# Three products of rounded parts in place of one fp32 product for the output projection of three batches

## The reference

```python
DIM, HEADS, DHEAD, CTX_DIM = (256, 16, 64, 192)
def _attn(x, ctx, Wq, Wk, Wv, Wo, bo):
    q = (x @ Wq).reshape(b, n, HEADS, DHEAD)
    ...
    attn = jax.nn.softmax(sim, axis=-1)
    out = jnp.einsum('bhij,bjhd->bihd', attn, v).reshape(b, n, INNER)
    return out @ Wo + bo
h = _ln(x, g1, be1)
x = _attn(h, h, Wq1, Wk1, Wv1, Wo1, bo1) + x
...
x = a * jax.nn.gelu(gate, approximate=False) @ W2 + b2 + x
```

## Time and profile before

| | us |
|---|---|
| median of 3 runs | 2043.34 (2043.1 to 2043.39) |
| the profiled execution | 2042.06 |
| its span | 2040.3 |

### The profile page before, as it was taken

One profiled execution on the slowest core, in us unless ns is written; L12 is line 12 of the kernel. 1 busy time (PEld: TensorE's weight loads), 2 busy tenths in 40 slices (PEclk: granted clock), 3 DMA queues, 4 the chain that ended last, 5 costly groups with the idle time before them and its releaser, 6 DMA issues.

```text
span 2040.3 us, 31825 instructions
## 1 busy us (share of the span) xinstructions
PE 2028.6 (99%) x12500; PEld 1387.7 (68%) x12500; DVE 1385.3 (68%) x2124; ACT 1159.7 (57%) x1851; POOL 1416.4 (69%) x745
## 2 busy tenths in 40 slices
PE   8999999999999999999999999999999999999999
PEld 7665665666565566665655666566558999888888
DVE  6477677666767785578678566757777898754453
ACT  5566577544557675255667544657665666533332
POOL 2699799975979998679799867979895576300000
PEclk9999999999999999999999999999999999999999
DMA  7300000001000000010000001000010530000100
GB/s 229 124 7 21 6 7 16 6 6 47 17 11 6 16 6 6 1 63 6 6 6 22 6 1 52 6 6 1 22 47 16 145 84 1 1 21 22 42 11 31
DMA packets 46566, 58.74 MB, mean 29 GB/s; under 512 B 5969, under 2 KB 40401, under 8 KB 45265
## 3 DMA queue, kind: packets, MB, share of 16 engines
q1 hardware_dynamic: 46416, 56.71, 8.9%
HBM read 38.88 MB, written 17.83 MB: 28 GB/s over the span
## 4 chain that ended last, share of the span: by engine, by line
PE 99%; ACT 1%; DVE 0%; DMA 0%; issue 0%; SPq 0%; ACTq 0%
PE score L494 22%; PE score L477 18%; PE score L603 9%; PE score L481 6%; PE score L425 5%; PE attn_project L617 4%; PE attn_project L589 4%; PE score L559 4%; PE attn_project L425 4%; PE first_score L451 4%; PE attn_project L528 3%; PE score L437 3%; PE score L528 2%; PE attn_project L451 2%; PE first_score L518 2%; PE attn_project L437 1%
## 5 line engine op out<-in xcount | busy, mean ns | idle before, releaser
L1316 POOL TENSOR_TENSOR acc<-acc,pT 128x1024 f32<-128x1024 f32 x384 | 914.6, 2382 | 55.4 <-POOL acc L1316 0.9
L1100 ACT ACTIVATE pT<-score 128x1024 f32<-128x1024 f32 x512 | 525.7, 1027 | 102.8 <-PE score L481 59.1
L477 PE MATMUL score<-qk 64*128 64x512 f32 x3072 | 456.2, 399 | 1.5 <-ACT oT L1111 0.9
L494 PE MATMUL score<-pT,vT 128*64 128x512 f32 x2016 | 446.5, 595 | 0.0
L780 DVE TENSOR_REDUCE nmax<-first_score 128x1 f32<-128x512 f32 x512 | 347.9, 679 | 3.5 <-PE first_score L451 1.4
L780 DVE TENSOR_REDUCE nmax<-attn_project 128x1 f32<-128x512 f32 x512 | 347.1, 678 | 0.0
L477 PEld LDWEIGHTS score<-qk 64*128 64x128 f32 x3072 | 257.1, 184 | 120.7 <-ACT pT L1100 67.9
L494 PEld LDWEIGHTS score<-pT,vT 128*64 128x64 f32 x2016 | 139.1, 137 | 289.4 <-issue 251.8
L1313 POOL TENSOR_TENSOR acc<-pT 128x1024 f32<-128x1024 f32 x64 | 154.0, 2406 | 150.3 <-ACT pT L1100 150.3
L802 DVE RECIPROCAL sums<-sums 128x512 f32<-128x512 f32 (+1 forms) x65 | 214.4, 3299 | 57.5 <-ACT sums L1125 56.9
L481 PE MATMUL score<-shift,pick 64*128 64x512 f32 x1024 | 205.5, 391 | 0.0
(11 more groups left out here) (160 smaller groups left out, 3056.1 us busy)
## 6 DMA issues: line engine op xcount, KB each, us to landing
xres<-x_middle SPq DMA_DIRECT2D x10, 512.0 KB, 3.7
xres<-in_x SPq DMA_DIRECT2D x4, 1024.0 KB, 7.6
raw_qk<-in_L_xattn_Wq SPq DMA_DIRECT2D x32, 128.0 KB, 2.2
raw_qk<-in_L_xattn_Wk SPq DMA_DIRECT2D x32, 128.0 KB, 2.4
raw_v<-in_L_xattn_Wv SPq DMA_DIRECT2D x8, 512.0 KB, 4.1
keys_all<-keys SPq DMA_DIRECT2D x1, 4096.0 KB, 12.1
values_all<-values SPq DMA_DIRECT2D x1, 4096.0 KB, 12.4
out_x<-xres SPq DMA_DIRECT2D x7, 512.0 KB, 2.9
```

Source lines behind the costliest of these rows:

```text
L477: e.matmul(bank, qk[P % 2][r, 2 + h, keys], qk[P % 2][r, w, queries], start=(part == 0), stop=False)
L494: last = e.matmul(banks[bank][head * DH:(head + 1) * DH, :], vT[:, v_slot(D, jt), c0:c0 + DH], pT[:, jt, head, :], start=(jt == 0), stop=( ...
L1100: e.activation(pT[:, jt].rearrange("p h n -> p (h n)"), SC[R % 2][:, :], ACT.Exp).then_inc(s.exponential, 1)
L1316: e.tensor_tensor(total, total, pT[:, jt], ALU.add).then_inc(s.probs_added, 1)
```

## The change

The output tiles of batches 0 to 2 are computed as three fp32r products of rounded parts, 24 products a tile in place of 8 in fp32. For that:

- `Wo1` is split once. ScalarE rounds a quarter of it in each of chunks 0 to 3 (`wo1_made`, in ring entries of `oT` that are not yet in use), VectorE subtracts (chunks 1 to 4) and leaves the rest in `wo1`'s own place. SP stores the rounded part in DRAM and loads it at the start of each later batch into `wv`, the place of the split value weights, which is free between two value projections; the second `split_wv` of a batch, in chunk n = 3, waits until the output tiles are done.
- The output's parts take the places of probabilities: `oT_parts[j]` for tile j of a slot are pT's tiles 0 and 1, 2 and 3, 4 and 5, and 0 and 1 again. ScalarE rounds (`split_oT`, three tiles ahead of `write_oT`, the fourth after the slot's other work and once tile 0 is multiplied). GpSimd subtracts, between its adds of the same chunk. Where the batch wraps round the ring a part is made in two pieces (`ring_pieces`).
- In the slot the output tiles now stand last, behind the qk projection.
- The last batch keeps the fp32 product (`out1_whole`), for which SP loads `Wo1` again.

```diff
@@ buffers
-            ("wo1", [PAIRS, DIM], F32))
+            ("wo1", [PAIRS, DIM], F32R))
+        _, *places = overlay(("oT_kept", [PRING, N], F32),
+                             *((f"oT_part{n}", [PAIRS, PART], F32R) for n in range(6)))
+        oT_parts = (places[0:2], places[2:4], places[4:6], places[0:2])
+        wo1_hi = wv[:, :, :, :].rearrange("p w k n -> p (w k n)")
...
+        _, wo1_made = overlay(("oT_first", [PRING - 2, N], F32), ("wo1_made", [PAIRS, DIM], F32R))
@@ slot
-            if b and n in (1, 2):
-                between += [("out1", b - 1, TPC * (n - 1) + t) for t in range(TPC)]
...
-            return jobs
+            return jobs + [("out1", *tile, through[i % len(through)]) for i, tile in enumerate(out1_tiles(C))]
+
+        def out1_tiles(C):
+
+            b, n = divmod(C, BC)
+            return [(b - 1, TPC * (n - 1) + t) for t in range(TPC)] if b and n in (1, 2) else []
+
+        def ring_pieces(b):
+
+            first = PAIRS * b % PRING
+            m = min(PAIRS, PRING - first)
+            return [(slice(first, first + m), slice(0, m))] + [(slice(0, PAIRS - m), slice(m, PAIRS))] * (m < PAIRS)
@@ TensorE
+            def out1(b, t, bank):
+                weights = (wo1_hi, wo1[:, :, :].rearrange("p q n -> p (q n)"))
+                need.wait_ge(s.wo1_hi, 16 * (b + 1))
+                need.wait_ge(s.wo1_lo, 4)
+                need.wait_ge(s.oT_hi, TILES * b + t + 1)
+                need.wait_ge(s.oT_lo, TILES * b + t + 1)
+                bank_free(bank)
+                for i, (o, w) in enumerate(TERMS):
+                    for p in range(PAIRS):
+                        last = e.matmul(banks[bank][:, 0:DIM], oT_parts[t % TPC][o][:, p, :],
+                                        weights[w][:, p * DIM:(p + 1) * DIM],
+                                        start=(i == p == 0), stop=(i == 2 and p == PAIRS - 1))
...
@@ ScalarE
+            def split_oT(C, b, t):
+
+                j = t % TPC
+                need.wait_ge(s.oT_scaled, BC * (b + 1) - (1 if t < TPC else 0))
+                need.wait_ge(s.attended, TILES * C + 2 * j + 1)
+                need.wait_ge(s.probs_added, (TILES - 1) * C + max(2 * j, 1))
+                if j == 3:
+                    need.wait_ge(s.out1_product, TILES * b + t - j + 1)
+                for there, pairs in ring_pieces(b):
+                    last = e.copy(oT_parts[j][0][:, pairs, :], oT[:, there, t * PART:(t + 1) * PART])
+                last.then_inc(s.oT_hi, 1)
...
+                if C < 4:
+                    split_wo1(C)
+                for tile in out1_tiles(C)[0:3]:
+                    split_oT(C, *tile)
                 write_oT(C)
                 whole_array(slot(C))
+                for tile in out1_tiles(C)[3:]:
+                    split_oT(C, *tile)
@@ GpSimd, split_wv
+                need.wait_ge(s.out1_product, D // 2 * TILES if D % 2 else 0)
@@ GpSimd
+            def split_oT(C, b, t):
+
+                j = t % TPC
+                hi, lo = oT_parts[j]
+                need.wait_ge(s.oT_hi, TILES * b + t + 1)
+                need.wait_ge(s.attended, TILES * C + 2 * j + 2)
+                need.wait_ge(s.probs_added, (TILES - 1) * C + 2 * j + 1 if j < 3 else 0)
+                for there, pairs in ring_pieces(b):
+                    last = e.tensor_tensor(lo[:, pairs, :], oT[:, there, t * PART:(t + 1) * PART],
+                                           hi[:, pairs, :].bitcast(F32), ALU.subtract)
+                last.then_inc(s.oT_lo, 1)
...
                 for jt in range(1, TILES):
                     add_probs(TILES * C + jt)
+
+                    for tile in out1_tiles(C)[{4: slice(0, 2), 5: slice(2, 3), 6: slice(3, 4)}.get(jt, slice(0, 0))]:
+                        split_oT(C, *tile)
@@ SP
+                if P == 2:
+                    need.wait_ge(s.wo1_made_a, 4)
+                    e.dma_start(wo1_dram, wo1_made[:, :, :].bitcast(F32).rearrange("p q n -> p (q n)")
+                                ).then_inc(s.wo1_stored, 16)
+                if P % PAIRS == 0 and b:
+
+                    need.wait_ge(s.wo1_stored, 16)
+                    need.wait_ge(s.v_projected, TILES * (GROUPS_B * b + 1))
+                    e.dma_start(wo1_hi.bitcast(F32), wo1_dram).then_inc(s.wo1_hi, 16)
...
+            need.wait_ge(s.out1_product, TILES * (B - 1))
+            e.dma_start(wo1_in[:, :, :], Wo1.rearrange("(q p) n -> p q n", p=PART)).then_inc(s.wo1_again, 16)
```

More of the change, by code:

```diff
@@ L24 @@
     ctx_copied wq2T_in_v keys2_v ln_stats ln_agg ln_rstd ln_rows ln_negated hT_full_v hT_lo split_lo row_max max_in
-    sum_inverse oT_scaled x1_added x2_added soft_max soft_sub soft_sum soft_inverse p2T_v gated u_lo y_added
+    sum_inverse oT_scaled oT_hi oT_lo wo1_made_a wo1_lo wo1_stored wo1_hi wo1_again x1_added x2_added soft_max soft_sub soft_sum soft_inverse p2T_v gated u_lo y_added
     ln_root ln_centred ln_rows_a hT_hi hT_full kv2_a wq2T_in keys2_a values2_a split_hi v_copied shift_in exponential oT_written sum_copied
@@ L132, in block_kernel @@
             ("wv", [2, KT, BANK], F32R),
-            ("wo1", [PAIRS, DIM], F32))
+            ("wo1", [PAIRS, DIM], F32R))
         qk = (qk0, qk1)
+        _, *places = overlay(("oT_kept", [PRING, N], F32),
+                             *((f"oT_part{n}", [PAIRS, PART], F32R) for n in range(6)))
+        oT_parts = (places[0:2], places[2:4], places[4:6], places[0:2])
+        wo1_hi = wv[:, :, :, :].rearrange("p w k n -> p (w k n)")
+        _, wo1_in = overlay(
+            ("kept_all", [(PRING + TILES) * N + TILES * BANK + (2 * ARING + 3) * BANK + 8 * N + PART
+                          + 10 * KT * PART + 3 * KT * BANK], F32), ("wo1_in", [PAIRS, DIM], F32))
+        _, wo1_made = overlay(("oT_first", [PRING - 2, N], F32), ("wo1_made", [PAIRS, DIM], F32R))
         (wkv2, wq2, wq2T, _, keys2, kv2, wo2, ctx_sb, ctxT) = overlay(
@@ L198, in block_kernel @@
                  "S1b": SC[1][:, BANK:], "T0": FS[:, 0:BANK], "T1": FS[:, BANK:], "PV": PX[:, 0:BANK], "PJ": PX[:, BANK:]}
+        wo1_dram = nc.dram_tensor("wo1_leading", (PART, PAIRS * DIM), F32, kind="Internal").ap()
         keys2_dram = nc.dram_tensor("keys2_all", (PART, B, KT * INNER), F32, kind="Internal").ap()
@@ L521, in sum_two, with out1_whole @@
                 free[bank] = ((s.sum_copied, C + 2),)
-            def out1(b, t, bank="PJ"):
+            def out1_whole(b, t, bank):
                 need.wait_ge(s.oT_scaled, BC * (b + 1) - (1 if t < TPC else 0))
-                need.wait_ge(s.wo1_loaded, 16)
+                need.wait_ge(s.wo1_again, 16)
                 bank_free(bank)
@@ L528, in out1 @@
                     last = e.matmul(banks[bank][:, 0:DIM], oT[:, (PAIRS * b + p) % PRING, t * PART:(t + 1) * PART],
-                                    wo1[:, p, :], start=(p == 0), stop=(p == PAIRS - 1))
+                                    wo1_in[:, p, :], start=(p == 0), stop=(p == PAIRS - 1))
+                last.then_inc(s.out1_product, 1)
+                free[bank] = ((s.x1_added, TILES * b + t + 1),)
+            def out1(b, t, bank):
[10 more added lines that the diff above has]
+                                        start=(i == p == 0), stop=(i == 2 and p == PAIRS - 1))
                 last.then_inc(s.out1_product, 1)
@@ L667, in _ @@
                 if i < TILES:
-                    out1(B - 1, i, last_out1(i))
+                    out1_whole(B - 1, i, last_out1(i))
                 if i == 1:
@@ L802, in invert_sums, with split_wo1 @@
                 e.reciprocal(sums[:, C % 2, part], sums[:, C % 2, part]).then_inc(s.sum_inverse, len(halves))
+            def split_wo1(q):
+                hi, lo = (w[:, 2 * q:2 * q + 2, :] for w in (wo1_made, wo1))
+                need.wait_ge(s.wo1_made_a, q + 1)
+                e.tensor_tensor(lo, wo1_in[:, 2 * q:2 * q + 2, :], hi.bitcast(F32), ALU.subtract).then_inc(s.wo1_lo, 1)
             def out1(b, t, bank="PJ"):
@@ L928, in _ @@
                     split_keys(1, 0)
+                if 1 <= C <= 4:
+                    split_wo1(C - 1)
                 if C >= 2:
@@ L1106, in write_oT @@
                 need.wait_ge(s.values2_stored, 16)
+                if P >= PRING - 2:
+                    need.wait_ge(s.wo1_stored, 16)
                 if P >= PRING:
@@ L1111, in write_oT, with split_wo1 @@
                 e.copy(oT[:, P % PRING, c * BANK:(c + 1) * BANK], banks["S0a" if C + 1 < NC else "PV"]).then_inc(s.oT_written, 1)
+            def split_wo1(q):
+                need.wait_ge(s.wo1_loaded, 16)
+                need.wait_ge(s.values2_stored, 16)
+                e.copy(wo1_made[:, 2 * q:2 * q + 2, :], wo1_in[:, 2 * q:2 * q + 2, :]).then_inc(s.wo1_made_a, 1)
+            def split_oT(C, b, t):
[8 more added lines that the diff above has]
+                last.then_inc(s.oT_hi, 1)
             def copy_sums(C, bank="PJ"):
@@ L1468, in _ @@
             load_wqk(1)
```

(2 more changed lines are left out.)

## The result

| | before | after |
|---|---|---|
| median of 9 runs, us | 2042.68 (2041.38 to 2043.39) | 2048.40 (2044.23 to 2049.64) |
| span of the profiled execution | 2040.3 | 2046.6 |
| TensorE's mean granted clock | 1.000 | 0.997 |

What follows compares the result with a forecast made beforehand. TensorE, busy 99% of the span, was taken to bound the kernel. Of 14.0 us, nine stay as waits on GpSimd at tile 3, so 5.0 gained: 2038.3 us, range 2031 to 2046.

Steps and rivals of the forecast that it cites:

- TensorE's part: Output-product slots on TensorE: tiles at 2.87 us, not 3.41, make a slot without waits 21.55 us, 2.33 less.
- The sum of 14.0: Six slots (24 tiles of batches 0 to 2) without any TensorE wait would give 14.0 us; chance of no waits 0.08.
- The weight loads: TensorE's loads hide beside 256-column products; the rival, loads in the open, 109 us slower at most, had chance 0.01.
- Prices on GpSimd and ScalarE: In the slots, a GpSimd rest costs 2.38 us, 0.23 more in two pieces; a ScalarE leading part 1.08, 0.16 more.
- The gap of 0.11: On GpSimd, an add needing the one before starts 0.11 us late; in the chain only rest 2 has such a neighbour.
- The slower rival: Tile 3 of all six slots: dear GpSimd rests; at 0.6 us more each, 9.1 us lost, 2052.4; chance 0.09.
- The chain on GpSimd: Rests between adds 4 to 7, counted from attend's start: rest 3 ends at 18.3 us (n = 1, batch 0), without wait.
- three signs that I set for being wrong: TensorE waits at tile 0, a rest differs from 2.4 and 2.6 by over 0.2, or chunks 16b+3 and later change length.
- The clock: Rival: TensorE's clock falls after a wait of up to 2.9 us; no price given, chance 0.02.
- The copies of the sums: Slot n = 2: ScalarE copies sums before leading parts, so GpSimd waits 3 us for leading part 0.
- Costs at nothing: Splitting Wo1, its DRAM store and loads, SP's waits, later copies to oT and the later value-weight split cost nothing.
- the mechanism of the sum: Six slots: TensorE's shorter work less its waits on GpSimd gains 5.2 us, 5.0 after hand-overs; chance 0.45 (gain 4.1 to 10).

## Why the prediction was wrong

By its own steps:

- *TensorE's part*: right. 2.33 a slot forecast, 2.3 measured in all six once nothing waits; 2.87 a tile forecast, 2.86 measured. The sum of 14.0 came as 13.9 (203.6 less 189.7). The weight loads stay beside the products at this shape, as the trace of before had it and against the rule of the Trainium skill's "TensorE: Matmul & The Clock Gate", section "The mechanism", that they overlap only when the row group differs. The same section excepts loads into "the background weight buffer"; whether the loads here are such, no run shows.
- *Prices on GpSimd and ScalarE*: right but for one gap. A leading part took 1.05, or 1.23 in two pieces. A rest took 2383 ns in one piece and 459 + 2108 = 2.57 in two, where 2.61 was taken, so strided reads cost nothing extra. The gap of 0.11 was too small: by its own row it is 0.13 (14.92 less six times 2.38, over five gaps), and in this place it is 0.17. By groups, in the changed kernel:

```profile
L1406 POOL TENSOR_TENSOR oT_part<-oT,oT_part 128x1024 fp32r<-128x1024 f32 x8 | 19.0, 2383 | 5.7 <-ACT oT_part L1176 5.3 <-POOL acc L1390 0.3
...
L1406 POOL TENSOR_TENSOR oT_part<-oT,oT_part 128x896 fp32r<-128x896 f32 x8 | 16.9, 2108 | 0.0
...
L1406 POOL TENSOR_TENSOR oT_part<-oT,oT_part 128x128 fp32r<-128x128 f32 x8 | 3.7, 459 | 5.9 <-ACT oT_part L1176 5.6 <-POOL acc L1390 0.3
```

  The slower rival as I put it, dear rests, is false.
- *The chain on GpSimd*: the step that failed. I wrote of slot n = 1 "ScalarE is idle then and its parts are ready", and of leading part 3 that it "waits for tile 0's product, A + 12.9, and is there by A + 14.3". It has a second wait, for add 6, in the diff that I showed. In n = 1 of batch 0 it came at A + 17.0. So 1.2 us of ScalarE and hand-over stood in series six times, and the n = 1 steps came 1.0 to 1.1 over the forecast each. TensorE's waits of over 0.15 in the six slots are 13.2 in all where 9 were forecast, and 6.2 in the first kernel, which has that wait loosened. None of the three signs that I set for being wrong came: tile 0 never waited, the rests had their price, the later chunks kept their length. None of them looked at tile 3, where the loss was.
- *The clock*: named as a rival, given 0.02 and no price. The argument against it was that TensorE had idled 3.3 us at the very start with the page at 9 tenths. That was a misreading. After that idle time and 0.71 more, the kernel before shows:

```profile
5.52 5.78 PE L369 MATMUL score<-ctxT,wkv 128*128 128x256 f32 x16 [0.71 <-DMA wkv<-in_L_xattn_Wk]
11.14 1.89 PE L369 MATMUL attn_project<-ctxT,wkv 128*128 128x256 f32 x8
12.87 3.77 PE L369 MATMUL score<-ctxT,wkv 128*128 128x256 f32 x16
```

  The first 16 products took 5.62 us, 0.35 each, the next eight 1.73, 0.22 each; record by record the step is 0.43 up to 9.5 us and 0.215 from 9.8 on. That is half the rate, as at the lower level, though the profile's clock value is 1.00 there too. And the page's digits hide a fall of 3 to 7 us in a slice of 51. The missed 1.2 us made the n = 2 waits 2.71, 2.93 and 2.93 us long, and the clock fell in each. Price: 5.4 us.
- *The copies of the sums*: right in mechanism. The idle 3.0 ahead of rest 0 was forecast at 3 and measured at 3.02 to 3.11. Alone it was worth about as much as the tight wait: without it the changed kernel is 14 us faster (2034.1), without the tight wait 12 (2036.0), clock included in both. With either of the two gone the clock stayed at 1.000, so its 5.4 needed both.
- *Costs at nothing*: right. All chunks outside the six slots stay within 0.1 us in sum. The value-weight split waited 4.8 us for the tiles in three places, and no one waited for it.

The account of the 11.3 us between the forecast span (2035.3) and the measured one, from the sums of the six steps: the missed wait is 7.4 (205.05 with the clock kept up, 197.64 with the wait loosened), the clock 5.3 (210.34 to 205.05, all six steps), the pieces of the chain were 0.9 cheaper than I took them (198.56, which is the step sum before less the 5.0, to 197.64), and the start was 0.5 shorter. With the wait mended and nothing else, the kernel gains 6.4 where 5.0 was forecast: the mechanism of the sum was sound but for this one wait, and the clock is a consequence of it.

What stays open: how long TensorE may wait before its clock falls. Waits of 1.7 left it, waits of 2.7 and 2.9 did not; nothing between was tried. Two waits of the same 2.93 cost 2.53 and 1.42, and the changed kernel's runs differ among themselves (mean clock 0.997 to 0.999, 2049.6 to 2044.2 us).

## What to carry to other kernels

Follow a chain across engines by each instruction's list of waits, every one with its count put into numbers, and not by what data it needs: a wait may be tighter than its reason, and a formula that is right for three values of j can be wrong for the fourth. A wait on TensorE that is long enough costs twice, once as idle time and once in the clock afterwards: here 1.2 us more of waiting cost 2.7 to 3.9 us in each n = 2 slot. When work moves onto an engine that is nearly full, look at the order in which its pieces stand between the old ones as well as at their price: here the rests were priced within 0.05 us, while moving rest 3 ahead of one add was worth 6.0 us and moving three roundings ahead of the copies 14.

## What the hardware showed that I had not expected

- A wait of TensorE of 2.71 to 2.93 us in the middle of steady work brought a stretch at 1.2 GHz that cost 1.4 us in two slots and 2.5 in one. With 1.53 to 1.7 us there was none.
- Ten useless products in front of the wait brought the clock back to 1.000 for the whole run, and took 5.4 us off the three n = 2 steps (4.5 off the median) without starting tile 3 any earlier.
- VectorE's split of `Wo1`, a subtraction of two SBUF operands over 512 elements, took 1913 ns in the mean of four (1.29 to 2.65 us), near the 2200 of the earlier trace rows, while GpSimd was adding in all four; on GpSimd the same form takes 1294. What makes it so slow and so uneven was not tested. By groups, in the changed kernel:

```profile
L846 DVE TENSOR_TENSOR wo<-wo_in,wo_made 128x512 fp32r<-128x512 f32 x4 | 7.7, 1913 | 0.0
...
L1341 POOL TENSOR_TENSOR w<-w_in,w 128x512 fp32r<-128x512 f32 x4 | 5.2, 1294 | 0.3
```
